# Decoder layer on one core: transposes of the up half, W2 and h moved from TensorE to a DMA queue, with the scaling and the rope sum divided anew

## The reference

```python
x = x + self_attn(layernorm(x))        # rope, 16 query heads in 4 groups, 4 kv heads of 16, causal softmax
x = x + cross_attn(layernorm(x), ctx)  # scores against ctx, masked softmax, readout of ctx
x = x + ffn(layernorm(x))

def ffn(x, w_gate_up, w_down):         # I = 704
    xq, w1q = quant_dequant(x, -1), quant_dequant(w_gate_up, -1)   # 8-bit steps by row maximum
    gate, up = split(xq @ w1q.T)
    h = silu(gate) * up
    return quant_dequant(h, -1) @ quant_dequant(w_down, -1).T
```

## Time and profile before

| | us |
|---|---|
| median of 3 runs (lowest, highest) | 102.81 (101.42, 103.00) |
| the profiled execution, device time | 101.47 |
| its span in the profile | 99.8 |
| busy: TensorE / VectorE / ScalarE / GpSimd | 90.2 / 75.7 / 65.7 / 66.1 |

### The profile page before, as it was taken

The page is one execution under the profiler, slowest core; times in us unless marked ns, Lnnn a source line. Parts: engine busy times, 40 slices in busy tenths (PEclk is TensorE's granted clock), DMA queues, the critical chain, the costliest instruction groups (busy, mean ns, idle before and its releaser), DMA issues.

```text
span 99.8 us, 2432 instructions
## 1 busy us (share of the span) xinstructions
PE 90.2 (90%) x804; PEld 68.8 (69%) x804; DVE 75.7 (76%) x217; ACT 65.7 (66%) x175; POOL 66.1 (66%) x136
## 2 busy tenths in 40 slices
PE   5999699999889999989999999979999999999560
PEld 4698467977576676767776777768778887775220
DVE  5046979957998988877896659797977788988731
ACT  1404216938839886776597878969986996988410
POOL 6266847975787977914638788848868962892220
PEclk9999999999999999999999999999999999999995
DMA  2999999940000000000000000000000010012121
GB/s 36 346 337 415 419 407 409 360 143 3 3 0 7 0 3 0 7 0 0 0 7 0 0 0 0 3 7 0 0 0 0 0 56 7 0 59 99 55 103 53
DMA packets 4521, 8.34 MB, mean 84 GB/s; under 512 B 349, under 2 KB 3358, under 8 KB 4382
## 3 DMA queue, kind: packets, MB, share of 16 engines
q1 hardware_dynamic: 4272, 7.96, 21.7%
q10 hardware_dynamic: 238, 0.23, 0.9%
HBM read 7.15 MB, written 1.05 MB: 82 GB/s over the span
## 4 chain that ended last, share of the span: by engine, by line
PE 72%; DVE 10%; POOL 7%; issue 5%; ACT 3%; DVEq 0%; POOLq 0%; ACTq 0%
PE ps_s L443 14%; PE ps_r L262 6%; PE ps_q L303 6%; PE ps_y L525 4%; PE ps_r L289 4%; PE ps_r L386 3%; PE ps_x L375 3%; PE ps_s L339 3%; PE ps_y L351 3%; PE ps_y L359 3%; PE ps_q L311 2%; PE ps_x L365 2%; DVE rot L846 2%; PE ps_s L469 2%; PE ps_y L354 2%
## 5 line engine op out<-in xcount | busy, mean ns | idle before, releaser
L1156 POOL TENSOR_TENSOR gate_up<-gate,up_row 128x704 f32<-128x704 f32 x7 | 11.9, 1698 | 3.7 <-ACT gate L723 3.5
L262 PE MATMUL ps_r<-warm 128*128 128x256 bf16 x60 | 9.4, 317 | 1.1 <-DVE warm L771 1.1
L262 PEld LDWEIGHTS ps_r<-warm 128*128 128x128 bf16 x60 | 6.7, 115 | 3.0 <-DVE warm L771 1.1
L1125 POOL TENSOR_TENSOR rot_c<-rot,b_rope 128x128 f32<-128x128 f32 x8 | 3.7, 459 | 7.5 <-DVE rot L846 7.5
L869 DVE RECIPROCAL y_rsum<-ps_y 128x128 f32<-128x128 f32 x8 | 7.6, 951 | 1.1 <-PE ps_y L354 1.0
L443 PE MATMUL ps_s<-gate_hi,x_int_T 128*128 128x352 f32 x28 | 7.5, 350 | 0.0
L1187 POOL TENSOR_TENSOR y_out<-ffn,x_aug 128x256 f32<-128x256 f32 x7 | 5.1, 729 | 3.7 <-DVE ffn L1025 3.7
L525 PE MATMUL ps_y<-w_T,h_T 128*128 128x256 bf16 (+1 forms) x42 | 6.5, 276 | 0.9 <-DVE ffn L1025 0.8
L443 PE MATMUL ps_s<-up_int,x_int_T 128*128 128x352 f32 x32 | 6.9, 337 | 0.0
L443 PE MATMUL ps_s<-gate_lo,x_int_T 128*128 128x352 f32 x28 | 6.8, 323 | 0.0
L610 ACT ACTIVATE p_self_T<-ps_s 128x512 f32<-128x512 f32 x8 | 4.8, 597 | 2.4 <-PE ps_s L339 2.4
(11 more groups left out here) (194 smaller groups left out, 285.8 us busy)
## 6 DMA issues: line engine op xcount, KB each, us to landing
ctxT<-in_ctxT SPq DMA_DIRECT2D x1, 1024.0 KB, 8.6
w_raw<-in_w SPq DMA_DIRECT2D x2, 512.0 KB, 11.0
ctx_aug<-in_ctx SPq DMA_DIRECT2D x1, 1024.0 KB, 17.0
out_x<-y_out SPq DMA_DIRECT2D x8, 128.0 KB, 1.7
x_aug<-in_x SPq DMA_DIRECT2D x1, 768.0 KB, 6.8
xT<-in_xT SPq DMA_DIRECT2D x1, 768.0 KB, 9.8
w_raw<-in_w SPq DMA_DIRECT2D x1, 704.0 KB, 14.6
x_first<-in_x_first SPq DMA_DIRECT2D x1, 416.0 KB, 4.3
```

Of the source, the lines that this page charges most:

```text
L262: nc.tensor.matmul(ps_r[:, 0:2 * T], warm[:, 0:P], warm[:, :], start=True, stop=True)
L1156: nc.gpsimd.tensor_tensor(gate_up[j % 2][:, :, :], gate[j % 2][:, :, :], up_row[:, :].rearrange("p (i f) -> p i f", i=2), ALU.mult).then_i ...
```

## The change

Three kinds of transposes go to SP's DMA queue: the up half of W1 in one transfer (128 x 1536 int16), W2 in two (128 x 768, the last 64 columns zeros) and h of batches 0 to 5 in one each (the same size). W2 and h are first cast from int16 to bf16 within SBUF by VectorE (`widen_w2`, `widen_h`, the latter waits until transpose j - 2 has landed). The up half lands as int16 and ScalarE casts it from SBUF. Batches 6 and 7 keep TensorE's transposes. The 13 scale columns of W1 and W2 are transposed by one TensorE instruction, copied by ScalarE, stored to DRAM and read back over all partitions. For batches 0 to 5 `scale_down` is divided: ScalarE multiplies the PSUM result by the row scale, GpSimd by `w2_row`. `rotate_sum` goes from VectorE to GpSimd, right behind `rotate_c`. All four lists are in new orders; there are 61 warming products where there were 60.

```diff
-    GT = -(-FF // P)
+    GT = FF // P
+    BY_DMA = 6
+    SPLIT = 6
...
+        w1_flat = w1_raw[:, :, :].rearrange("p o d -> p (o d)")
+        UT = (WT - GT) * DC * P // 2
+        up_T = w1_flat[:, 0:UT].bitcast(I16).rearrange("p (o c t) -> p o c t", c=DC, t=P)
+        padded = w1_flat[:, UT:UT + 2 * FC * P].bitcast(BF16).rearrange("p (i f) -> p i f", f=FC * P)
+        w2_bf = padded[:, 0:DC]
+        h_bf = [padded[:, DC + i] for i in range(2)]
...
+            done(sp, "w1_int_ready", 4)
+            sp.dma_start_transpose(up_T[:, :, :, :].rearrange("p o c t -> p (o c) t"),
+                                   w1_int[:, GT:WT, :].rearrange("p o d -> p (o d)")).then_inc(s["up_T_loaded"], 16)
+            done(sp, "scale_rows_ready", 0)
+            sp.dma_start(scale_rows_dram, scale_rows[:, :]).then_inc(s["scale_rows_stored"], 16)
+            sp.wait_ge(s["scale_rows_stored"], 16)
+            sp.dma_start(out_rows[:, :], scale_rows_dram.rearrange("o p -> (o p)")[FF:2 * FF + D].unsqueeze(0).to_broadcast([P, FF + D])).then_inc(s["rows_loaded"], 16)
+            done(sp, "pads_zero", 0)
+            for c in range(DC):
+                done(sp, "w2_bf_ready", c)
+                sp.dma_start_transpose(w2_T[:, :, c * P:(c + 1) * P], w2_bf[:, c, :]).then_inc(s[f"w2_T_{c}_loaded"], 16)
+            def transpose_h(j):
+                done(sp, "h_bf_ready", j)
+                if j >= 2:
+                    done(sp, "down_done", j - 2)
+                sp.dma_start_transpose(h_T[j % 2][:, :, :], h_bf[j % 2]).then_inc(s[f"h_T_{j}_loaded"], 16)
+            def store_out(j):
+                if j < LAST:
                     done(sp, "y_out_ready", j)
                 else:
                     done(sp, "last_y_out_ready", 0)
                 sp.dma_start(out[j], y_out[:, j, :]).then_inc(s["out_stored"], 16)
+            transpose_h(0)
+            transpose_h(1)
+            transpose_h(2)
+            transpose_h(3)
+            transpose_h(4)
+            store_out(0)
+            transpose_h(5)
+            store_out(1)
+            store_out(2)
+            store_out(3)
+            store_out(4)
+            store_out(5)
+            store_out(6)
+            store_out(7)
...
+            def transpose_scales(last, k):
...
+                nc.tensor.transpose(ps_r[0:WT + DC, 0:P], w_scale[:, :], ident[:, :]).then_inc(s["scales_transposed"], 1)
...
+                    for c in range(DC):
+                        pe.wait_ge(s[f"w2_T_{c}_loaded"], 16)
+                if j >= 1 and j - 1 < SPLIT:
+                    done(pe, "down_scaled", j - 1)
+                elif j >= 1:
+                    done(pe, "ffn_ready", j - 1 - SPLIT)
+                if j < BY_DMA:
+                    pe.wait_ge(s[f"h_T_{j}_loaded"], 16)
+                else:
+                    done(pe, "h_T_ready", j - BY_DMA)
...
+            project_out(5); scores(7); transpose_cross_p(4); weigh_values(6); transpose_x1(5)
+            transpose_q_max(7); readout(4, "x2_ready", 3); score_keys(7); cross_scores(5)
+            transpose_x_int(2, "x2_ready", 4); project_out(6); gate_product(0); weigh_values(7)
+            transpose_x_int(3, "x_int_T_ready", 2); transpose_cross_p(5); up_product(0); transpose_x1(6)
+            readout(5, "x_int_T_ready", 3); cross_scores(6); gate_product(1); project_out(7)
+            transpose_x_int(4, "x2_ready", 5); transpose_cross_p(6); transpose_x1(7); up_product(1)
+            cross_scores(7); gate_product(2); transpose_cross_p(7); readout(6, "x_int_T_ready", 4)
+            up_product(2); transpose_x_int(5, "x2_ready", 6); gate_product(3); readout(7, "x_int_T_ready", 5)
+            gate_product(4); transpose_x_int(6, "x2_ready", 7); up_product(3); gate_product(5); down(0)
+            up_product(4); gate_product(6); down(1); up_product(5); transpose_x_int(7, "x_int_T_ready", 6)
+            down(2); up_product(6); last_gate(0); down(3); last_gate(1); up_product(7); down(4); transpose_h(6)
+            down(5); down(6); last_transpose_h_a(); last_transpose_h_b(); last_down_a(); last_down_b()
 
...
+            def evacuate_up(c):
+                act.wait_ge(s["up_T_loaded"], 16)
+                nc.scalar.copy(up_int[:, c, 0:FL], up_T[:, 0, c, FL:P])
+                nc.scalar.copy(up_int[:, c, FL:FF].rearrange("p (o t) -> p o t", t=P), up_T[:, 1:WT - GT, c, :]).then_inc(s["up_int_ready"], 1)
+            def copy_scales():
+                done(act, "scales_transposed", 0)
+                nc.scalar.copy(scale_rows[:, :], ps_r[0:WT + DC, 0:P]).then_inc(s["scale_rows_ready"], 1)
...
+            def scale_down_rows(j):
+                free(act, "y_out_ready", j, 3)
+                done(act, "down_done", j)
+                nc.scalar.mul(ffn[j % 3][:, :], ps_y[:, 0:D], h_scale[:, j:j + 1]).then_inc(s["down_scaled"], 1)
...
+            upper_gate(2); evacuate_x1(1); evacuate_q_max(3); evacuate_up(0); exp_self(3); copy_scales()
+            evacuate_qk(4); exp_cross(1); square_1(2); evacuate_cross_p(1); square_2(0); evacuate_up(1)
...
+            silu_gate(2); evacuate_cross_p(7); evacuate_x_int(5); quantise_h(0); silu_gate(3); quantise_x(6)
+            quantise_h(1); silu_gate(4); evacuate_x_int(6); quantise_h(2); square_2(6); silu_gate(5)
+            quantise_x(7); scale_down_rows(0); quantise_h(3); silu_gate(6); scale_down_rows(1); quantise_h(4)
+            evacuate_x_int(7); square_2(7); scale_down_rows(2); quantise_h(5); scale_down_rows(3); last_silu(0)
+            last_silu(1); quantise_h(6); scale_down_rows(4); evacuate_h(6); scale_down_rows(5)
+            last_quantise_h(0); last_quantise_h(1); last_evacuate_h_a()
...
+            def widen_w2(c):
+                if c == 0:
+                    done(dve, "w1_int_ready", 4)
+                    nc.vector.memset(padded[:, :, FF:], 0.0).then_inc(s["pads_zero"], 1)
+                done(dve, "w2_int_ready", c)
+                nc.vector.tensor_copy(w2_bf[:, c, 0:FF], w2_int[:, c, :]).then_inc(s["w2_bf_ready"], 1)
...
+            def widen_h(j):
+                if j >= 2:
+                    dve.wait_ge(s[f"h_T_{j - 2}_loaded"], 16)
+                done(dve, "h_int_ready", j)
+                nc.vector.tensor_copy(h_bf[j % 2][:, 0:FF], h_int[j % 2][:, :]).then_inc(s["h_bf_ready"], 1)
...
+            amax_h(1); amax_x(6); scale_h(1); invert_h(1); step_x(6); invert_x(6); widen_h(0); hidden(2)
+            residual_2(7); amax_h(2); widen_h(1); amax_x(7); scale_h(2); invert_h(2); hidden(3)
+            step_x(7); invert_x(7); amax_h(3); widen_h(2); scale_h(3); invert_h(3); hidden(4); amax_h(4)
+            widen_h(3); scale_h(4); invert_h(4); hidden(5); amax_h(5); widen_h(4); scale_h(5); invert_h(5)
+            hidden(6); widen_h(5); amax_h(6); last_widen(0); scale_h(6); invert_h(6); last_widen(1)
+            last_hidden(0); last_amax_h(0); last_hidden(1); last_amax_h(1)
+            last_scale_h(); scale_h(7); invert_h(7); scale_down(6); last_evacuate_h_b(); scale_down(7)
+            add_residual(7)
...
+            def rotate_sum(j):
+                if j == 0:
+                    pool.wait_ge(s["zeros_ready"], 6)
+                free(pool, "q_max_transposed", j, 3)
+                done(pool, "rot_done", j)
+                done(pool, "rot_c_done", j)
+                nc.gpsimd.tensor_tensor(
+                    qk_rot[j % 3][:, :, :, 0:DH].rearrange("p i h (t f) -> p t (i h) f", t=2),
+                    rot_c[j % 3][:, :, :].rearrange("p t (n f) -> p t n f", f=F),
+                    rot[j % 3][:, 3:1:-1, :].rearrange("p t (n f) -> p t n f", f=F), ALU.add).then_inc(s["qk_ready"], 1)
...
+            def weigh_down(j):
+                done(pool, "down_scaled", j)
+                nc.gpsimd.tensor_tensor(ffn[j % 3][:, :], ffn[j % 3][:, :], w2_row, ALU.mult).then_inc(s["ffn_weighed"], 1)
...
+            rstd_2(6); widen_gate(0); whole_x2(5); scale_x(4); rstd_2(7); widen_gate(1); scale_x(5)
+            widen_gate(2); widen_gate(3); whole_x2(6); whole_x2(7); widen_gate(4); scale_x(6); widen_gate(5)
+            weigh_down(0); widen_gate(6); add_residual(0); scale_x(7); weigh_down(1); add_residual(1)
+            weigh_down(2); weigh_down(3); add_residual(2); weigh_down(4); add_residual(3); weigh_down(5)
```

279 lines of the change are left out of this document (104 added, 175 removed).

## The result

The changed kernel takes 97.01 us, the median of four runs (96.50 to 98.23); the kernel before took 102.12 in the same comparison, and the ratio of the two is 0.956, with a 95% interval of 0.948 to 0.964. The profiled execution of after took 96.63 us with a span of 94.9, that of before 101.47 with 99.8: 4.84 us less.

What follows compares the result with a forecast made beforehand. TensorE was taken to bound the kernel from 30 us on. Removing 6.7 us of its work, less 1.7 of new waits, gives 5.0 us: 102.8 becomes 97.8 us, range 94.8 to 102.2.

Steps and rivals of the forecast that it cites:

- likeliest case: Whole kernel: the first rival, 97.8 us with its own range of 95.5 to 100.2; chance 0.60.
- Part 1: TensorE: scale spreads and transposes of the up half, W2 and six h leave, saving 6.7 us in full stages.
- Part 5: DMA path of h: a transpose takes 3.0 us; new waits of TensorE, with ScalarE's 0.2, cost 1.7 us.
- Part 3: VectorE: 7.7 us leave, eight casts at 0.40 bring 3.2; net 4.5 less, which only removes lateness.
- Part 4: GpSimd: eight rope sums (3.7 us) and six weighings (4.4 us) come in, covered because its adds can lag.
- The cover: GpSimd in the late stage: its work fits before the last scale_down may run, with about 5 us to spare.
- Part 2: ScalarE: six h evacuations go, six scaled evacuations at 0.38 come; net about 1.8 us less work.
- second rival: Late stage: another engine bounds it; casts of 0.87 add 2.8 us to VectorE's queue, time 100.8; chance 0.17.
- Third rival: SP's queue: transposes of h run one at a time, making the kernel slower, 107.6 us at 4 us each; chance 0.13.
- D: SP's queue: time of each serial transpose of h; from 3.2 us the end passes the present 97.65.
- Fourth rival: TensorE: layout work sat in time it would have waited in, so no change, 102 us; chance 0.10.
- a wash: Rope sum: GpSimd's 0.46 us replaces VectorE's 0.42 with the same wait for rot_c, so no latency change.

Runs made afterwards that it cites:

- experiment 4: The changed kernel with all down products scaled by VectorE in one operation again, not by ScalarE and GpSimd: 0.954 of before, lowest run 96.49 us.
- experiment 8: The changed kernel without GpSimd's multiplications of batches 0 to 5 by W2's scales: 0.947 of before, lowest run 95.82 us.
- experiments 1: The changed kernel with six groups of six unread TensorE transposes added in the late stage: 0.955 of before, median 97.85 us, lowest run 96.69.
- experiment 2: The changed kernel with the transposes of x1 of batches 3 to 7 done twice on TensorE: 0.960 of before, lowest run 97.30 us.
- experiment 12: The changed kernel with the orders of experiment 11 and h of batch 5 transposed by TensorE, evacuated by ScalarE: median 95.19 us, 0.940 of before.
- experiment 11: The changed kernel with the last batch's second gate product and both its silu operations moved ahead of down(3) and its scaling: 96.61 to 100.11 us, no ratio.
- experiment 7: The changed kernel with each DMA transpose of h done twice, first into a spare place: 0.994 of before, lowest run 100.77 us.

## Why the prediction was right

**The time.** 97.8 was forecast and 97.01 measured, in the range of 94.8 to 102.2 and in the likeliest case's own; 5.0 us of gain against 4.84 between the profiled executions and 5.1 between the medians. Of the 0.8 us between forecast and result, 0.7 is the median of before, 102.81 in the runs shown and 102.12 beside the changed kernel.

**Part 1, 6.7 us off TensorE:** 7.0 by the busy sums. Right, and the term that carries the result.

**Part 5 and the waits, 1.7 us:** 2.1 more by the lists of waits and by the idle time as a whole, but not where I put them. Of the 1.2 us of waits for `h_T` in `down(2)`, `(3)` and `(4)` there is 0.5, once, in `down(3)`; landing was 2.7 us for the 3.0 taken. Silu cost 0.8 and not 0.45. What I didn't list are 0.6 for `hid` by the up products, 1.0 for `h_int` of batch 6 (before, the list has 0.4 for that of batch 7 in its place) and the `down` that waits for ScalarE's scaled evacuation, 0.6, which takes the place of 0.8 for VectorE's. The sum was near by errors that cancel.

**Part 3, VectorE 4.5 less:** 2.3 less. The casts of h were mis-sized: 0.60 in the mean for 0.40, because GpSimd holds them up; undisturbed they take 0.33, below my value, and those of W2 took 0.28 and 0.58. That is 1.3 us in place of the forecast 3.2 becoming 4.5. The two products of gate and scale of the last batch took 0.74 for 0.53 and 0.56 in before, another 0.4. The formula of the page "VectorE: DVE Perf Modes" of the Trainium skill that the prediction used, 58 + 704/4 cycles, would give an estimated 0.24; its section "The TRN2 errata — SBUF-src ops pay a fixed extra latency per instruction" says that this formula is too low for a single operation and that the fixed part measured about 150 cycles, which would be an estimated 0.34. The trace has 0.28 and 0.33 undisturbed, between the two.

**Part 4, GpSimd:** 8.5 us more against 8.1; the weighing took 0.78 and the rope sum 0.456. The cover is thinner than "about 5 us": the add of batch 4 is the first of three from 89.23 on and ends near 89.9, and the last scaling of a down product starts at 91.76, so some 1.8 are left. It held in so far as the time is the same with all of the scaling on VectorE (experiment 4); without the weighings it is 0.7 lower (experiment 8).

**Part 2, ScalarE 1.8 less:** 2.8 less. The scaled evacuation took 0.47 for 0.38, but the remainders that I left uncounted went as well.

**What bounds it.** "From 30 us on an instruction taken off TensorE shortens the kernel" fits the gain, 4.9 us for 7.0, and is weaker in the changed kernel. There some 2.1 us more of TensorE's work in the late stage cost 0.2 by the lowest runs and 1.3 by the positions in the profile, and some 1.1 us more in the attention part cost 0.8 (experiments 1 and 2). The second rival (another engine bounds the late stage) happened in part: it added 2.8 us to VectorE with six casts of 0.87, where 0.60 in the mean added 1.2, and taking one such cast and its DMA transpose away gave 1.2 us at the last batch (experiment 12). That the price was small enough to leave the gain is what the forecast had right.

**Third rival.** D was 2.7, under its point of 3.2, and one holds the queue for 1.21 us of its 2.7. That was the usual landing: the one of batch 5 took 3.2 in after and 4.3 in experiment 11, beyond the point of 3.2. Doubling the transposes gave back 4.3 of the 4.8 us, part of it by the clock (experiment 7). The estimate of 7.85 us for one h adds up six blocks at the 1309 ns that the same page of the Trainium skill gives for one in its section "The three transpose paths". The trace doesn't have that sum: six blocks of 128x128 landed together in 2.7 us. **Fourth rival:** excluded by 7.0 us less work and just 2.1 more idling.

**The rope sum.** I called its move a wash. It is worth 0.5 to 1.0 us, since VectorE and not TensorE paces the stretch from 10 to 30 us. The trace of before had it already: TensorE has holes there, and from 10 to 57 us its longest entry among the waits is for this very sum.
```profile
PE ps_q L311 <- DVE qk_rot L856: 1.4, 4, 0.6
```

## What to carry to other kernels

When one engine's work is taken away, the row to watch is when its neighbours fill up: more of the same then buys only a part of what is taken off, and work belongs into the gaps of whichever engine still has them, batch by batch, as one h back on TensorE showed (1.4 us). A latency path through a DMA queue is cheap as long as what lies between the producer and the consumer is longer than cast, issue and landing together; count that slack with the latest landing and not the median one (4.3 against 2.7 us here), since a late one can cost the clock as well. Price a load that you add by what it moves its engine's list on, not by the length of one record: for the transposes of experiment 2 that is 0.11 us each and not 0.27. And price a short VectorE operation by what GpSimd does in the same moment.
